# The product of probabilities and values: one float32 matmul a block, or two float32r matmuls on split operands

## The reference

```python
q, k, v = split_heads(x @ wq.T) * s, split_heads(x @ wk.T) * s, split_heads(x @ wv.T)
q, k = rope(q), rope(k)
attn = softmax(einsum('bhtd,bhld->bhtl', q, k) + causal_mask)
out  = einsum('bhtl,bhld->bhtd', attn, v)          # the product that the change rewrites
x1   = layernorm(x + out.reshape(B, T, D) @ wo.T)
h    = gelu(concat(x1, stats(x1)) @ r1_w.T + r1_b)  # its argument: 128 "hidden" rows, one column a token
probs = softmax(h @ r2_w.T)                         # the router
```

## Time and profile before

| | |
|---|---|
| median of 3 runs | 2577.28 us (2570.64 to 2580.52) |
| span of the profiled execution | 2586.7 us |
| attention | 0 to about 1602 us |
| route | about 1602 to 1880 us |
| experts | about 1880 to 2500 us |
| last norm | to the end |
| TensorE matmul busy | 2069.4 us, 80% |
| VectorE busy | 1516.8 us, 59% |
| ScalarE busy | 1338.2 us, 52% |
| TensorE's mean granted clock | 0.88 of full speed |

### The profile page before, as it was taken

The page is one execution under the profiler, slowest core; times in us unless marked ns, Lnnn a source line. Parts: engine busy times, 40 slices in busy tenths (PEclk is TensorE's granted clock), DMA queues, the critical chain, the costliest instruction groups (busy, mean ns, idle before and its releaser), DMA issues. The chain is left out here.

```text
span 2586.7 us, 45555 instructions
## 1 busy us (share of the span) xinstructions
PE 2069.4 (80%) x14340; PEld 1866.9 (72%) x14340; DVE 1516.8 (59%) x3366; ACT 1338.2 (52%) x3381; POOL 793.3 (31%) x889
## 2 busy tenths in 40 slices
PE   6899997899997799997899985311568888888880
PEld 5799886798886698886798874301457887888880
DVE  6555666555665455666556663688745455454444
ACT  5566664566664566664466543000455455555545
POOL 1122241222331122242101111000755555555543
PEclk9899998899997799997899976555889899999995
DMA  1000001000010000001000002000023333444327
GB/s 57 13 18 18 26 27 32 17 18 18 26 32 28 19 18 18 26 26 31 13 14 20 20 25 82 0 0 0 0 75 109 120 112 117 133 119 128 110 48 260
DMA packets 79907, 127.51 MB, mean 49 GB/s; under 512 B 15652, under 2 KB 69904, under 8 KB 75628
## 3 DMA queue, kind: packets, MB, share of 16 engines
q1 hardware_dynamic: 63852, 114.99, 12.8%
q0 software_dynamic: 15872, 10.24, 2.7%
HBM read 100.29 MB, written 35.65 MB: 53 GB/s over the span
## 5 line engine op out<-in xcount | busy, mean ns | idle before, releaser
L458 PE MATMUL out_ps<-v_sb,probs_t 128*128 128x64 f32 x4352 | 559.5, 274 | 46.1 <-DVE probs_t L749 35.7
L458 PEld LDWEIGHTS out_ps<-v_sb,probs_t 128*128 128x128 f32 x4352 | 540.5, 196 | 55.8 <-DVE probs_t L749 52.8
L735 DVE TENSOR_REDUCE part_max<-scores_ps 128x1 f32<-128x512 f32 (+3 forms) x576 | 357.3, 622 | 299.0 <-PE scores_ps L426 233.9
L426 PE MATMUL scores_ps<-k_st,q_parts 128*128 128x512 f32 (+3 forms) x1280 | 418.9, 411 | 23.5 <-POOL q_parts L863 14.2
L605 ACT ACTIVATE probs<-scores_ps,neg_max 128x512 f32<-128x512 f32 (+3 forms) x640 | 397.4, 626 | 61.0 <-DVE neg_max L739 46.7
L614 ACT COPY probs_t<-probs_t_ps 128x512 f32<-128x512 f32 (+3 forms) x416 | 208.7, 502 | 282.6 <-PE probs_t_ps L443 281.5
L443 PE MATMUL probs_t_ps<-ident,probs 128*128 128x128 f32 x2176 | 352.7, 278 | 2.3 <-DVE probs_t L749 2.2
L443 PEld LDWEIGHTS probs_t_ps<-ident,probs 128*128 128x128 f32 x2176 | 265.3, 144 | 54.4 <-issue 6.4
L1457 PE MATMUL up_ps<-xe_t,w 128*128 128x320 f32 x1920 | 289.1, 310 | 2.3 <-DVE xe_t L1564 1.7
L1457 PEld LDWEIGHTS up_ps<-xe_t,w 128*128 128x128 f32 x1920 | 283.8, 189 | 2.9 <-issue 1.9
L426 PEld LDWEIGHTS scores_ps<-k_st,q_parts 128*128 128x128 f32 x1280 | 207.6, 200 | 37.0 <-issue 16.3
(11 more groups left out here) (219 smaller groups left out, 3229.8 us busy)
## 6 DMA issues: line engine op xcount, KB each, us to landing
w_raw<-in_w_expert SPq DMA_DIRECT2D x32, 1536.0 KB, 6.4
w_raw<-in_w_adapter SPq DMA_DIRECT2D x32, 384.0 KB, 6.8
x_t<-in_x_t SPq DMA_DIRECT2D x64, 128.0 KB, 2.1
x_row<-in_x SPq DMA_DIRECT2D x64, 128.0 KB, 2.0
x_rows<-x SPq DMA_DIRECT2D x64, 128.0 KB, 1.7
acc_rows<-x SPq DMA_DIRECT2D x64, 128.0 KB, 1.8
ln_x<-acc_rows SPq DMA_DIRECT2D x16, 512.0 KB, 6.2
out_rows_dram<-ln_y SPq DMA_DIRECT2D x16, 512.0 KB, 5.2
```

The costliest lines, as they stand in the source:

```text
L426: mm = pe.matmul(out, q_parts[:, s % 2, part_, h, :], k_st[:, h, lo:hi], start=part_ == 0, stop=part_ == 1 and not diagonal)
L458: mm = pe.matmul(o_ps[:, h, :], probs_t[:, g % PT_RING, a - lo:a - lo + P], v_sb[:, a // P, h, :], start=a == 0, stop=a == t * P)
L735: red = dve.tensor_reduce(neg_max[:, ring:ring + 1] if single else part_max[:, ring, c:c + 1], s_ps[:, bank[g], 0:hi - lo], AX.X, ALU.max, ...
```

## The change

Values are stored as a float32r upper part and the remainder (`v_sb` has 2 x 64 columns a head), and so are the transposed probabilities (`probs_t` has two planes). Per block of 128 keys there are two float32r matmuls: upper probabilities by both parts of the values (128 columns), and the remainder of the probabilities by the upper part of the values (64 columns), added to the first 64 columns. ScalarE now writes the upper part of every chunk; VectorE then subtracts it from `t_ps` for every chunk (`lower_probs`). The two halves of `o_ps` are added in `norm`, which has three VectorE instructions in place of one. Values get a remainder on VectorE too (`lower_v`), and ScalarE's reading of `ot` waits for it. The hidden rows go to a small SBUF ring and from there to DRAM; `route` loads them back into `hpre`.

```diff
-        o_ps = ctx.enter_context(nc.psum_tensor("out_ps", [P, HEADS, HD], F32))
+        o_ps = ctx.enter_context(nc.psum_tensor("out_ps", [P, HEADS, 2 * HD], F32))
-        v_sb = sb("v_sb", [P, NT, HEADS, HD])
+        v_sb = sb("v_sb", [P, NT, HEADS, 2 * HD], F32R)
-        probs_t = sb("probs_t", [P, PT_RING, CH])
+        probs_t = sb("probs_t", [P, PT_RING, 2, CH], F32R)
...
+            def store_hidden(i, k):
+
+                wait(sp, hid_copied, ONE + NT // 2 * i + k // 2 + 1, sp_passed)
+                sp.dma_start(dram["hidden"][:, bass.ds((i * NT + NT - 1 - k) * P, 2 * P)], hidden[:, k // 2 % 2, :])\
+                  .then_inc(hid_stored[k // 2 % 2], 16)
...
-                    if g >= 2:
-                        o = owner[g - 2]
-                        pe.wait_ge(probs_copied[o], ONE + copies[o] * i + nth[g - 2] + 1)
...
+                    pe.wait_ge(probs_split, ONE + CHUNKS * i + max(g - 1, 0))
...
                     for a in range(lo, hi, P):
-                        mm = pe.matmul(o_ps[:, h, :], probs_t[:, g % PT_RING, a - lo:a - lo + P],
-                                       v_sb[:, a // P, h, :], start=a == 0, stop=a == t * P)
+                        at = slice(a - lo, a - lo + P)
+                        pe.matmul(o_ps[:, h, :], probs_t[:, g % PT_RING, 0, at], v_sb[:, a // P, h, :],
+                                  start=a == 0, stop=False)
+                        mm = pe.matmul(o_ps[:, h, 0:HD], probs_t[:, g % PT_RING, 1, at], v_sb[:, a // P, h, 0:HD],
+                                       start=False, stop=a == t * P)
...
-                            act.wait_ge(v_proj, n + 1)
+                            act.wait_ge(v_copied, ONE + n + 1)
...
+            def lower_v(out_ps, n, t):
+                dve.wait_ge(v_upper, n + 1)
+                dve.tensor_tensor(v_sb[:, t, :, HD:2 * HD], out_ps.rearrange("p (h d) -> p h d", h=HEADS),
+                                  raw(v_sb[:, t, :, 0:HD]), ALU.subtract).then_inc(v_copied, 1)
...
+                def lower_probs(g):
                     lo, hi = keys(g)
...
+                    dve.wait_ge(probs_upper, CHUNKS * i + g + 1)
+                    dve.tensor_tensor(probs_t[:, g % PT_RING, 1, 0:hi - lo], t_ps[:, g % 2, 0:hi - lo],
+                                      raw(probs_t[:, g % PT_RING, 0, 0:hi - lo]), ALU.subtract)\
+                       .then_inc(probs_split, 1)
...
-                        dve.tensor_tensor(attn[:].rearrange("p (h d) -> p h d", h=HEADS), o_ps[:],
-                                          norm_by[:, r].to_broadcast([P, HEADS, HD]), ALU.mult).then_inc(attn_ready, 1)
+                        heads = attn[:].rearrange("p (h d) -> p h d", h=HEADS)
+                        dve.tensor_copy(heads, o_ps[:, :, HD:2 * HD])
+                        dve.drain()
+                        dve.tensor_tensor(heads, o_ps[:, :, 0:HD], heads, ALU.add)
+                        dve.drain()
+                        dve.tensor_tensor(heads, heads, norm_by[:, r].to_broadcast([P, HEADS, HD]), ALU.mult)\
+                           .then_inc(attn_ready, 1)
...
+            for b in range(NTT // 16):
+                for g in range(G):
+                    part = slice((g * TG + 4 * b) * P, (g * TG + 4 * b + 4) * P)
+                    sp.dma_start(hpre[:, part], dram["hidden"][:, part]).then_inc(hid_loaded[b], 16)
...
+                act.wait_ge(hid_loaded[b], 16 * G)
```

More of the change, by code:

```diff
@@ L151, in attention_slots, with attention @@
     return units, chunks, banks, products, early, late, aside, bank, former
-def attention(nc, dram, NB, NT, hpre):
+def attention(nc, dram, NB, NT):
     S = NT * P
@@ L236, in attention @@
         squares = sb("squares", [P, D])
+        hidden = sb("hidden", [P, 2, 2 * P])
         part = sb("part", [P, 1])
@@ L339, in body @@
                         store(i - 1, NT - 2 + s)
+                    if s % 2 == 0:
+                        if s >= 4:
+                            store_hidden(i, s - 3)
+                        elif not is_first(i):
+                            store_hidden(i - 1, NT - 3 + s)
             batches(sp, body)
@@ L343, in _ @@
                 store(NB - 1, s)
+            for k in (NT - 3, NT - 1):
+                store_hidden(NB - 1, k)
             for r in range(2):
                 sp.wait_ge(x1_stored[r], 32 * (NT // 2) * NB)
+                sp.wait_ge(hid_stored[r], 16 * (NT // 4) * NB)
         @block.tensor
@@ L528, in _ @@
         def _(act):
-            for semaphore in (exp_done, hid_copied, qk_copied, v_copied, q_copied, probs_copied[1]):
+            for semaphore in (exp_done, hid_copied, qk_copied, q_copied):
                 act.sem_inc(semaphore, ONE)
@@ L626, in main @@
                     exps(g + 2, g + AHEAD)
-                    if g < CHUNKS and owner[g] == 1:
+                    if g < CHUNKS:
                         copy(g)
@@ L672, in step @@
                         act.wait_ge(hid_done, NT // 2 * i + k // 2 + 1)
-                        act.copy(hpre[:, bass.ds((i * NT + t) * P, 2 * P)], m_ps[:, D:2 * D]).then_inc(hid_copied, 1)
+                        j = k // 2
+                        if j >= 2 or not is_first(i):
+                            act.wait_ge(hid_stored[j % 2], 16 * (NT // 4 * i + j // 2))
+                        act.copy(hidden[:, j % 2], m_ps[:, D:2 * D]).then_inc(hid_copied, 1)
                 act.wait_ge(q_copied, ONE + NT * (i + 1))
@@ L754, in main @@
                         maximum(g + AHEAD)
-                    if g < CHUNKS and owner[g] == 0:
-                        copy(g)
+                    if g < CHUNKS:
+                        lower_probs(g)
                 def step(kind, k, i, more):
@@ L823, in step @@
                                           ALU.subtract).then_inc(x1_split, 1)
+                    elif kind == "v_read" and more:
+                        lower_v(misc("v", k)[:, D:2 * D], n, t)
                     elif kind == "rope" and more and ("proj", k) in aside:
@@ L913, in rope_sums, with route @@
     return eng.tensor_tensor(roped[:, :, 0, :, 1], products[:, 2], products[:, 3], ALU.add)
[L916 to L923, removed]
+def route(nc, dram, NTT, cap, slot_token, slot_weight, w_raw, w_loaded):
     G = P // E
@@ L984, in route @@
         tok_f = sb("tok_f", [P, COLS])
+        hid_loaded = [sem(f"hid_loaded{b}") for b in range(NTT // 16)]
         loaded, consts, cleared = sem("route_loaded"), sem("route_consts"), sem("route_cleared")
@@ L1688, in build @@
         dram[name] = nc.dram_tensor(f"{name}_rows", (T, D), F32).ap()
+    dram["hidden"] = nc.dram_tensor("hidden_cols", (HID, T), F32).ap()
     with ExitStack() as ctx:
@@ L1692, in build @@
         w_loaded = [ctx.enter_context(nc.semaphore(f"w_loaded{r}")) for r in range(2)]
[L1693 to L1694 removed]
+        attention(nc, dram, NB, NT)
         w_raw = ctx.enter_context(nc.sbuf_tensor("w_raw", [P, 2, W], F32))
[L1696 removed]
+        route(nc, dram, NTT, cap, slot_token, slot_weight, w_raw, w_loaded)
         experts(nc, dram, T, cap, slot_token, slot_weight, w_raw, w_loaded)
```

27 lines of the change are left out of this document (10 added, 17 removed).

## The result

The changed kernel takes 2779.6 us (median, 2778.3 to 2785.1) against 2578.5 of the kernel before beside it: a ratio of 1.078, 95% interval 1.076 to 1.080. The profiled execution spans 2777.1 us, 190.4 more than before's.

What follows compares the result with a forecast made beforehand. Attention was taken as bound by TensorE for about three quarters of a batch, by chains between engines otherwise. 0 + 136 (path) + 2 (projection) + 6 (route) = 144 us on 2577.3 gave 2721 us, range 2615 to 2800.

Steps and rivals of the forecast that it cites:

- TensorE's price, 0: Values product: the same 4352 loads and records at 0.113 us each, so TensorE's own time is unchanged.
- The rival in which columns set the price: Values product: columns, not weight loads, set the price; 272 us off, 2313 us; chance 0.06 of a part that shows.
- VectorE's load: Attention: some 320 us more VectorE work, 85%, 86%, 85% and 64% busy with 4, 3, 2 and 1 chunks.
- What of it lies on the path: Attention: delays of 1.5, 2, 3 and 2 us a tile with 4, 3, 2, 1 chunks, 136 us for four batches.
- The tile's end: Statistics to next tile, 2 chunks a head: a subtraction ahead and longer `norm` make TensorE 1.5 to 2.2 us late.
- Values and `ot`: ScalarE's reads of values and `ot`: a subtraction and two hand-overs between them delay TensorE's `wo` by 0.6 us a tile.
- Projection tiles: First batch's 16 projection tiles: `lower_v` between rope and the k remainder costs 0.1 us a tile, 2 us.
- TensorE's waits ahead of the product: Sign of being right: TensorE's waits ahead of the values product well over 100 us, for the subtraction and `norm`.
- Route: End of attention: the first Gelu waits for the last hidden row's store and loads, 6 us later (4 to 10).
- The rival's price of 108 us: Stage with 2 chunks: new gaps drop the clock to 0.72, 108 us over four batches, 2829 us; chance 0.12.
- VectorE fits in: Attention: VectorE's new work falls into its waits; only `norm` in short tiles and route remain, 40 us, 2617; chance 0.24.

Runs made afterwards that it cites:

- later_both: The changed kernel with the values product and `norm` each one chunk later where a head has 2 or more chunks; 2816.8 us, ratio 1.093.
- norm_one: The changed kernel with `norm` as one VectorE instruction on the upper half of the sums, the other half left out; 2710.2 us, ratio 1.049.
- sub_first: The changed kernel with VectorE's subtraction for chunk g put ahead of the maximum for chunk g + 4; 2997.7 us, ratio 1.164.

## Why the prediction was right, and where it was off

The forecast was slower, at 2721 us in a range of 2615 to 2800. Measured were 2779.6: +201 where +144 was the sum, near the upper end of the range. The direction and its cause were right. The size came in the range with some luck: the values' hand-over was priced too high, most stages too low, and the clock wasn't in the sum at all. By its steps:

- **TensorE's price, 0.** Right at full clock. 0.22 to 0.23 us a block against 0.225, and with VectorE's new work taken out TensorE is as full as before. The rival in which columns set the price is out.
- **VectorE's load.** 1812 us against 1840 forecast; right in kind and near in size. By stage of the third batch it is 101.6, 84.8, 63.4 and 55.5, where 108.5, 85.5, 63.6 and 54.2 were forecast. The 85% was taken over the old length of a stage; over the new one it is 71% to 74%.
- **What of it lies on the path, 136.** This is the term that was mis-sized: the last hidden row comes 186.8 us later, of which 1.2 arise ahead of the first batch's attention, so about 186 stand where 136 were taken. The stages of a batch grew by 10.4, 15.8, 15.2 and 4.9 us on average, where 6, 8, 12 and 8 were taken. I sized it by one tile with 2 chunks and went down from there, as TensorE is a step further from needing the subtraction. This slack protects a stage less than I took it to: the stages with 3 chunks were twice as dear as forecast, and in later_both one more step of slack helped those with 2 chunks, but not those with 3 and 4.
- **The tile's end, 1.5 to 2.2 us late.** Right in place: 4.96 in place of 3.95 us on VectorE, TensorE idle for 1.60. norm_one measures `norm`'s part as 69 us, 1.1 a tile, about all of the 1.0 us by which its work and drains grew.
- **Values and `ot`, 0.6 a tile.** The hand-over measured 0.65, but taking it out gave 10 us in all, not 38.
- **Projection tiles, 2 us.** The first transposes of probabilities began 1.2 us later (94.2 and 95.4): right.
- **TensorE's waits ahead of the product, well over 100 us.** 54.6 for the subtraction and 47.4 for `norm`, 102 in all: over 100, but not well over. They were 35.7 and 9.8, so they grew by 56 of the 187 us. The rest of the 187 shows in other waits and in the longer busy time.
- **Route, 6 us (4 to 10).** 7.3 in the trace: right.
- **The clock.** The sum had nothing for it. The rival's price of 108 us didn't come: in the stage with 2 chunks it fell to 0.94, and to 0.79 in the fourth batch, not to 0.72. But a part of its mechanism did, up to 56 us by the estimate above. The kernel before shows the price in its own runs: of the twelve beside norm_one the slowest spans 2587.5 us at a granted clock of 0.881 and the fastest 2567.5 at 0.890, 20 us for 51 us more at half clock (twice the share missing from 1, times the span). By this price, about 0.4, the 112 us make some 44. So the clock is a quarter to three tenths of the 187, by estimate. It comes with the stalls; no run holds it fixed.
- **VectorE fits in, 2617.** Out, with TensorE's waits at 54.6 and 47.4.

What I had wrong in the picture: I counted what TensorE waits for directly, the product above all. VectorE's queue also holds the maxima, which release the exponentials and through them the transposes and the next scores. The new duration delays all of them. That the exponentials' wait grew from 47 to 113 us is shown, and sub_first makes the maxima later still, though it leaves VectorE idle besides. How the 156 us divide between late subtractions, late maxima and the clock isn't settled: no run delays one without the others.

## What to carry to other kernels

Before a float32 product with few columns is split into float32r parts, look whether the price of a record moves with its columns at all. Here it is 0.11 us a record at full clock, averaged over a block, whether both have 64 columns or one 128 and one 64, and the split keeps the number of loads. Cost new work on an in-order engine by who waits behind it, not by its busy share: 295 us more on an engine at 59% cost 190. A pure load of 225 cost 38, a short instruction in the chain 38, the full instruction in the chain, 335 us of load, 156, and two instructions at a tile's end were three times as dear on the loaded engine (69 us against 20). Where the new stalls break up TensorE's work, look at the granted clock as well: it was a part of the price here that no wait shows.

## What the runs showed that I had not expected

- Giving the product one chunk more slack made the kernel 119 us slower, as another in-order instruction (`norm`) then waited 51.7 us ahead of urgent work. With `norm` later too, the stages with 2 chunks took 20 us less, and those with 3 and 4 chunks 59 more.
- Of the 187 us in attention only 87 are idle time of TensorE. The rest is the same 10336 matmuls counted busy for longer, at a lower clock and in shorter runs.
- Of the 0.22 us of a float32r block, 0.14 lie ahead of the 64-column record and 0.08 ahead of the 128-column one; with equal columns before, nearly all were 0.11 apart. The sum is the same. At half clock it is 0.25 and 0.17, and 0.21 twice before.
- Swapping two VectorE operations that stand next to each other cost 218 us, more than the whole change.
